# Latent projections in 128x32 tiles beside the values, in another PSUM bank; two ScalarE copies reordered

## The reference

```python
x = x + attention(layernorm(x))             # 16 local heads of 16, plus a latent branch
x = x + cross(layernorm(x), ctx)            # 16 heads, causal, then a layer norm with gamma, beta
x = x + slots(layernorm(x))                 # 64 slots, top 8, one GRU step
# the latent branch of the first attention:
pooled = xn.reshape(B, 64, 2, D).mean(axis=2)
rq = xn @ rq_w + rq_b                       # 4 heads of 16
rk, rv = split(pooled @ rkv_w + rkv_b)
remote = softmax(mask(rq @ rk.T / 4)) @ rv @ rout_w + rout_b
gate = sigmoid(local @ gl_w + remote_h @ gr_w)
out = (gate * local + (1 - gate) * remote_h) @ out_w + out_b
```

## Time and profile before

| What | Value |
|---|---|
| Median of 3 runs | 1458.13 us (1457.26 to 1459.05) |
| The profiled execution's own time | 1459.16 us |
| Its span | 1457.4 us |
| PE busy | 1394.8 us, 96% of the span |
| DVE busy | 1063.9 us, 73% |
| ACT busy | 895.6 us, 61% |
| POOL busy | 847.1 us, 58% |

### The profile page before, as it was taken

The page is one execution under the profiler, slowest core; times in us unless marked ns, Lnnn a source line. Parts: engine busy times, 40 slices in busy tenths (PEclk is TensorE's granted clock), DMA queues, the critical chain, the costliest instruction groups (busy, mean ns, idle before and its releaser), DMA issues. The chain is left out here.

```text
span 1457.4 us, 57196 instructions
## 1 busy us (share of the span) xinstructions
PE 1394.8 (96%) x22238; PEld 1061.1 (73%) x22238; DVE 1063.9 (73%) x3000; ACT 895.6 (61%) x1573; POOL 847.1 (58%) x1177
## 2 busy tenths in 40 slices
PE   6999999999999999997999999999999959999997
PEld 4777777777777777765777777777777736776775
DVE  6666676666776667763677777777777768999996
ACT  3555655556555555553676666767666538877874
POOL 3566555666555665553477877777777743443442
PEclk9999999999999999997999999999999969999999
DMA  6500000000000000002100000000000000110111
GB/s 170 155 2 1 0 0 0 0 0 0 0 0 0 0 0 0 1 2 86 42 17 22 14 22 14 21 15 14 22 14 14 3 1 15 37 36 29 36 36 44
DMA packets 31207, 32.40 MB, mean 22 GB/s; under 512 B 3937, under 2 KB 29602, under 8 KB 31138
## 3 DMA queue, kind: packets, MB, share of 16 engines
q1 hardware_dynamic: 31138, 31.46, 7.1%
HBM read 23.06 MB, written 8.39 MB: 22 GB/s over the span
## 5 line engine op out<-in xcount | busy, mean ns | idle before, releaser
L1073 POOL TENSOR_SCALAR_AFFINE_SELECT a_probs_t<-a_probs_t 128x512 f32<-128x512 f32 x256 | 162.3, 669 | 38.8 <-ACT a_probs_t L709 37.5
L1619 DVE TENSOR_REDUCE c_neg_max<-score_banks 128x8 f32<-128x512 f32 (+1 forms) x128 | 116.5, 952 | 82.8 <-PE score_banks L1352 82.8
L1784 POOL TENSOR_SCALAR_AFFINE_SELECT c_probs_t<-c_probs_t 128x512 f32<-128x512 f32 x256 | 153.9, 636 | 15.6 <-ACT c_probs_t L1546 15.6
L709 ACT ACTIVATE a_probs_t<-score_banks 128x2048 f32<-128x2048 f32 x64 | 120.3, 1879 | 41.2 <-PE score_banks L554 41.2
L1546 ACT ACTIVATE c_probs_t<-score_banks 128x2048 f32<-128x2048 f32 x64 | 120.3, 1879 | 26.2 <-PE score_banks L1380 26.2
L397 PE MATMUL side_banks<-a_xn_t,a_w_qk 128*128 128x256 f32 x512 | 133.8, 396 | 1.6 <-ACT a_xn_t L654 0.7
L856 DVE TENSOR_REDUCE a_neg_max<-score_banks 128x8 f32<-128x512 f32 (+1 forms) x128 | 116.3, 950 | 7.7 <-PE score_banks L524 7.7
L825 DVE TENSOR_TENSOR v_heads<-side_banks,a_b_v 128x272 f32<-128x272 f32 x64 | 27.9, 437 | 117.0 <-issue 102.5
L1095 POOL TENSOR_TENSOR a_less<-a_attn,a_remote 128x512 f32<-128x512 f32 x31 | 39.5, 1273 | 113.2 <-DVE a_attn L879 113.2
L2212 POOL TENSOR_TENSOR r_hn<-rz_t,half_hn 128x256 f32<-128x256 f32 x32 | 23.3, 728 | 139.3 <-ACT rz_t L2040 139.3
L698 ACT ACTIVATE a_remote<-side_banks 128x544 f32<-128x544 f32 x32 | 20.0, 625 | 134.3 <-PE side_banks L484 134.3
(11 more groups left out here) (271 smaller groups left out, 3982.6 us busy)
## 6 DMA issues: line engine op xcount, KB each, us to landing
x_sb<-in_x SPq DMA_DIRECT2D x32, 256.0 KB, 3.1
ctx_in<-in_ctx SPq DMA_DIRECT2D x32, 256.0 KB, 2.7
out<-y SPq DMA_DIRECT2D x32, 256.0 KB, 2.1
w_ih<-in_ffn_w_ih SPq DMA_DIRECT2D x1, 768.0 KB, 4.6
w_hh<-in_ffn_w_hh SPq DMA_DIRECT2D x1, 768.0 KB, 6.0
a_raw_qk<-in_attn_qk_w SPq DMA_DIRECT2D x1, 512.0 KB, 4.4
a_raw_cross<-in_xattn_qk_w SPq DMA_DIRECT2D x1, 512.0 KB, 4.6
b_ih<-in_ffn_b_ih SPq DMA_DIRECT2D x1, 384.0 KB, 6.8
```

Of the source, the lines that this page charges most:

```text
L709: nc.scalar.activation(probs_t[tt][:].rearrange("p h q -> p (h q)"), score_banks[:].rearrange("p b n -> p (b n)"), ACT.Exp, scale=SCALE).t ...
L1073: nc.gpsimd.affine_select(out=probs, in_=probs, pattern=[[0, 4], [1, 128]], compare_op=ALU.is_ge, fill=0.0, base=-1, channel_multiplier=-1 ...
L1619: ins = nc.vector.tensor_reduce(neg_max[:, tt, :].rearrange("p (i s l) -> p i s l", i=4, s=2)[:, :, :, late], all_scores[:, :, :, 128 * (1 ...
L1784: nc.gpsimd.affine_select(out=heads, in_=heads, pattern=[[0, 4], [1, 128]], compare_op=ALU.is_ge, fill=0.0, base=0, channel_multiplier=-1) ...
```

## The change

`project_lat` is split in two. Its queries and keys are now computed in tiles of 128 rows by 32 columns, four side by side (16 matmuls where there were 8), and run just before `values(prev, 0)`; the latent values follow `values(prev, 0)` as `project_lat_values`. `lat_bank` moves from `av_bank` to `q_bank`, so `project_lat` waits for `evac_q`, `project_v(at, 1)` waits for all three operations of `evac_lat`, and `max_transpose(prev, 1)` no longer waits for `evac_lat`. DVE runs `evac_lat` later, right before `bias_v(at, 1)`. On ACT `copy_lat_t` goes ahead of `copy_max(prev, 1)`. In the cross attention ACT runs `evac_av(prev, 0)` ahead of `copy_xn(following)`.

```diff
@@ banks
-    lat_bank, latT_bank, lo_bank = av_bank, back_bank, (av_bank, back_bank)
+    lat_bank, latT_bank, lo_bank = q_bank, back_bank, (av_bank, back_bank)
@@ project_lat
-                wait(pe, maxT_ready, at.count(2, -1))
+                pe.wait_ge(q_ready, at.count(1, 1))
...
+                for src, lo, to, n in ((xn_t, 0, 256, S), (pooled, HALF, 384, LAT)):
+                    for c in range(C):
+                        for tt in range(2):
+                            for hh in range(0, HALF, 32):
+                                pe.matmul(lat_bank[HALF * tt + hh:HALF * tt + hh + 32, to:to + n],
+                                          w_lat[:, c, lo + hh:lo + hh + 32], src[:, c, n * tt:n * tt + n],
+                                          start=(c == 0), stop=(c == C - 1), skip_group_check=True)
+
+            def project_lat_values(at):
                 for c in range(C):
                     mm = pe.matmul(lat_bank[:, 448:512], pooled[:, c, :], w_v[:, c, VW:],
@@ project_v, second half
-                    pe.wait_ge(q_ready, at.count(1, 1))
+                    pe.wait_ge(lat_ready, at.count(3, 3))
@@ max_transpose, second
-                elif more(at):
-                    pe.wait_ge(lat_ready, at.count(3, 6))
@@ PE step
-                    project_lat(at)
                     project_q(at, 1)
...
                     scores_t(prev, 1)
+                if at.real:
+                    project_lat(at)
                 if prev.real:
                     values(prev, 0)
+                if at.real:
+                    project_lat_values(at)
                 if following.real:
                     transpose_x(following)
@@ ACT step
+                    copy_lat_t(prev)
                     copy_max(prev, 1)
-                    copy_lat_t(prev)
@@ DVE step: evac_lat(at) from ahead of x_scale(following) to ahead of bias_v(at, 1)
@@ cross attention, ACT step
                     copy_ctx(following)
+                if prev.real:
+                    evac_av(prev, 0)
+                if following.real:
                     copy_xn(following)
-                if prev.real:
-                    evac_av(prev, 0)
```

More of the change, by code:

```diff
@@ L970, in step @@
                     gate_logits(old)
-                if at.real:
-                    evac_lat(at)
                 if following.real:
@@ L984, in step @@
                 if at.real:
+                    evac_lat(at)
                     bias_v(at, 1)
@@ L1575, in step @@
                     copy_ctx(following)
-                    copy_xn(following)
                 if prev.real:
                     evac_av(prev, 0)
+                if following.real:
+                    copy_xn(following)
             copy_ctx(At(0, 0))
```

## The result

| What | Before | Changed |
|---|---|---|
| Median | 1458.59 us (1457.26 to 1459.57) | 1471.3 us (1471.18 to 1473.74) |
| Ratio, 95% interval | | 1.0091 [1.0076, 1.0106] |
| Span of the profiled execution | 1457.4 us | 1469.5 us |

The direction was right, the size was not: +12.7 us where +6.0 was predicted, and 0.3 us over the top of the range.

The account below looks back on a forecast made before the run. PE, busy for 96% of the span, was taken to bound the kernel. First attention +11.5 us and cross attention -5.5 us gave +6.0 us: 1458.1 + 6.0 = 1464.1 us, range 1452 to 1471 us.

Parts of the forecast that it names:

- the pair's price: First attention: one pair's stretch grows from 7.60 to 7.97 us, +0.37 us, times 31 pairs: +11.5 us.
- Everything behind that is untouched: First attention on PE: work after the start of the second `project_v` was taken to keep its time.
- L397's filling: First attention on PE: L397 was taken to need 0.92 us from start to start.
- the wait on ACT: Ahead of `lat_values`: PE ready at s + 2.42 us, starts at s + 2.91, 0.49 us later, needing L686 and L703.
- the wait on DVE: Second `project_v` waits for L819 to empty the latent bank: 0.29 us, bounds 0.2 and 0.4.
- The stretch: PE from the group after `scores_t(prev, 0)` to the second `project_v`: 7.60 us before, 7.97 us forecast.
- s: Start on PE of the group after `scores_t(prev, 0)`, from which the first attention's times are counted.
- The short tiles: Latent keys in 128x32 tiles, four rounds of N=64: 0.23 us; rival of 0.11 us a round, 1470.6 us, chance 0.10.
- The estimate from the 60 cycles: Latent keys' 16 records at the skill's minimum per matmul: 0.40 us, stretch 0.17 us more, kernel about 1470 us.
- POOL: First attention: L1106, which L589 needs, ends at s + 7.05, L589 comes at s + 7.24: no cost, 0.1 us to spare.
- Wait on ACT not felt: First attention: L703 ends by s + 2.3 us, stretch 7.48 us, kernel 1449 us; chance 0.10.
- The cross attention: Stall ahead of L1407 goes, 0.24 us; DVE limits every second pair to 0.12: mean 0.18, -5.5 us by 31 pairs.

Follow-up runs that it names:

- the first run: Kernel before with only the cross attention's order on ACT changed (evac_av(prev, 0) ahead of copy_xn(following)): 1455.1 us, ratio 0.9972 [0.9961, 0.9984].

## Why the prediction was wrong

Two steps failed. The account of a pair ended with "Everything behind that is untouched", and L397's filling was taken from its old neighbours: the pair grew by 0.48 us, not by 0.37. And the pair's price was multiplied by 31 with nothing for the ends of the stage, where 4.1 us more were lost. Both new waits came as forecast.

**Point by point, steady pair.** The means of the 20 pairs, beside the terms of the prediction:

| Term | Predicted | Measured |
|---|---|---|
| L397 ahead of the latent transposes | 0.92 | 0.967 |
| L461 and L535 | 0.49 | 0.493 |
| L441 to L473, with the wait on ACT | 1.50 | 1.477 |
| L473, L545, L551 | 1.71 | 1.710 |
| Latent queries and keys, 128x32 | 0.69 | 0.684 |
| L567 | 0.99 | 0.987 |
| L428, L391 | 0.94 | 0.938 |
| L586, with the wait on DVE | 0.73 | 0.746 |
| The stretch | 7.97 | 8.001 |
| Second L441 behind it | 0.92, as before | 1.021 |
| L594 | 1.86, as before | 1.820 |

- The stretch of before was 7.59 us in the mean, so it grew by 0.41 us where 0.37 was predicted. The mechanisms were right: both new waits are there, at the places named. L473 starts at s + 2.94 in the mean (2.91 predicted), the second `project_v` at s + 8.00.
- **The wait on ACT** was split wrongly: L441 with its change of shape costs 1.07, not 1.01 us, and the wait 0.41, not 0.49. Of the earlier trace rows's 1.20 us less was waiting than I took (0.13, not 0.19). The sum of the two held, 1.48 against 1.50, since ACT's chain sets when L473 starts, whatever the group ahead of it costs.
- **L397** lost its neighbour in the same shape (L429) and now starts behind L551's 32x128 tiles. It takes 0.05 us more to fill. The prediction took its 0.92 from the old neighbourhood.
- **The wait on DVE**: its place was right to 0.01 us (L819 ends 1.64 us after L428 starts, 1.56 taken; L441 comes 1.68 after it, 1.67 taken). What failed is the sentence "Everything behind that is untouched": the second L441 itself needs 0.10 us more from start to start when its first weights come late, and L594 gives back 0.035. So this wait costs 0.37 us a pair, not 0.29. The run with the values early shows it, where all three terms return at once (L586 0.437, L441 0.919, L594 1.855 us).
- Together +0.48 in place of +0.37 us a pair, 15.0 in place of 11.5 us.
- **The short tiles** went as forecast: 16 records of the keys within 0.22 us. The estimate from the 60 cycles for each matmul of the Trainium skill (TensorEngine Tiling (Array Packing), Performance Considerations, Instruction Overhead) was 0.40 us; the trace does not agree for tiles that run side by side.
- **POOL** cost nothing, with 0.09 us to spare. With the exponential halved, PE is earlier and L391 ahead of L586 takes 0.479 us where it took 0.443: a small price that the rival "Wait on ACT not felt" left out.
- **The cross attention** gave 6.3 us where 5.5 were predicted. That every second pair gives less was right (14.78 and 14.95 us against 15.02 and 15.10), and L1352 ahead of L1407 takes 0.82 to 0.84 us with the new order where it took 1.05. That DVE is what takes part back is not shown. L1374 does start only 0.07 us after DVE's maximum in every second pair, but the group ahead of it takes 0.96 us before and after. The time comes back earlier in the pair: L1396 goes from 1.04 to 1.09 us, with POOL's masks named as its releaser, and in the first run L1364 goes from 0.13 to 0.24 us.

**The term that was missing.** The largest error, some 4 us, is in none of the terms: PE stands in `values` in pairs at both ends of the stage. The prediction multiplied a steady pair by 31, but five of the 31 steps are written out and two more are the loop's first round. In favour of a late supply of instructions: no semaphore is missing; instructions are read by DMA in 30 to 130 us and not at all in 400 to 600 us; with half as many latent matmuls little is lost; and where PE stood longest, nothing but instructions was read, and nine packets more than in the two other executions of that kernel. At 56 to 60 us x is being loaded as well, so there the loads of x are not excluded; at 290 to 300 us they are. Against a simple price for each written-out pair: two of the six pairs are in the loop, and the kernels with 8 and 16 more written-out pairs ran most of these without loss, one at 1465.37 us. The reads of 30 to 130 us are nearly as many in the kernel before (13 packets of 16 KB, 14 in the changed one), so their number doesn't decide; that the 128x32 group is the densest stretch of instructions, 32 matmul records ahead of `values`' 32, is my reading and was not shown by itself. That instructions come too late is the likely cause, argued and not shown. Why `values`, and why so different from run to run, stays open.

The terms add up: 6.0 predicted, +3.5 steady pair, +4.1 at both ends of the stage, -0.8 cross attention, -1.1 at the start, +0.4 between and behind: 12.1 us, the difference of the spans.

## What to carry to other kernels

Work taken from in front of an engine that waits for another is not saved, it was the cover of that wait: write down for each operation moved what it hid, and when its bank's next user comes. A wait on PE can cost more than its idle time: the one on DVE also made the group behind it 0.10 us longer, the one on ACT did not (L473 0.38 us with it and without). And a pair of the loop times the number of pairs isn't the kernel: read the first pairs and the last ones by themselves. The best version here is the cross attention's new order alone, 0.28% faster than the kernel before and, by the two ratios, 1.2% faster than the changed one.

## What the runs showed of the hardware

- A change of tile shape makes the group ahead of it about 0.10 us longer from start to start (keys in 128x64 tiles 0.33 us with a change behind them, in 128x32 tiles without one 0.22) and the group behind it up to 0.05 us (L397 0.919 to 0.967); a full group with a change behind it takes 1.07 us where 0.92 is its own.
- 128x32 tiles with N = 64, four side by side, start 16 records in 0.22 us, 14 ns each.
- One and the same kernel with more PE instructions written out took from 1465 to 1537 us. In the execution at 1481 us a single pair took 29.27 us instead of 20.6: PE idle for 6.3 us at the start of the loop's second round with only instruction reads on the DMA queues, and the granted clock at 1.2 GHz for the 7 us behind it.
